# First phase of an adaLN transformer layer on Trainium2: what is loaded when, V projected four chunks behind Q and K, squares in four buffers

## The reference

```python
mod = (_silu(L0_c) @ L0_wmod).reshape(L0_c.shape[0], 6, 1, -1)
sa, ca, ga, sb, cb, gb = (mod[:, 0], mod[:, 1], ...)
h = _layernorm(x, axis=-1) * (1 + ca) + sa
q = hidden_states @ Wq + bq     # k, v alike; 8 heads of 128
scores = einsum('bhqd,bhkd->bhqk', q, k) / sqrt(HD);  attn = softmax(scores)
attn_out = attn @ v1 - lam * (attn @ v2)     # v1, v2: value heads 0..3 and 4..7
...
x = x + ga * _L0_attn_ref(h, ...)
x = x + gb * _L0_ffn_ref(_layernorm(x) * (1 + cb) + sb, ...)
```

## Time and profile before

| | |
|---|---|
| median of the runs shown | 2617.07 us (2615.12 to 2673.77, 3 runs) |
| the profiled execution | 2620.93 us |
| its span on the slowest core (core 3) | 2619.4 us |
| spans of the other cores | 2603.2 to 2617.3 us |
| TensorE busy | 2381.9 us, 91% of the span |
| VectorE, ScalarE, GpSimd busy | 27%, 54%, 12% |
| mean granted TensorE clock, core 3 | 0.971 of full speed |
| first score matmul, core 3 | 249.14 us |

### The profile page before, as it was taken

One profiled execution on the slowest core, in us unless ns is written; L12 is line 12 of the kernel. 1 busy time (PEld: TensorE's weight loads), 2 busy tenths in 40 slices (PEclk: granted clock), 3 DMA queues, 4 the chain that ended last, 5 costly groups with the idle time before them and its releaser, 6 DMA issues.

```text
span 2619.4 us, 43310 instructions; the slowest of 8 cores (2603.2 to 2619.4 us)
## 1 busy us (share of the span) xinstructions
PE 2381.9 (91%) x17364; PEld 1332.5 (51%) x17364; DVE 701.5 (27%) x1231; ACT 1422.8 (54%) x1551; POOL 319.1 (12%) x278
## 2 busy tenths in 40 slices
PE   1788999999989899989899995679999999999999
PEld 0343666655656565656566663334444444444444
DVE  2653121121222211122236666621020110201101
ACT  1333888978879688978887774451302113021120
POOL 1111000000000000000035453321010100101000
PEclk9999999999999899999999998899999999999999
DMA  9630101111011100000446666791020111202101
GB/s 219 143 97 1 22 9 26 22 25 22 9 25 21 25 5 9 5 9 7 71 106 142 146 149 174 188 210 52 33 81 17 65 33 49 81 14 67 33 33 41
DMA packets 119507, 162.74 MB, mean 62 GB/s; under 512 B 37696, under 2 KB 86924, under 8 KB 118288
## 3 DMA queue, kind: packets, MB, share of 16 engines
q1 hardware_dynamic: 79440, 119.60, 14.7%
q0 software_dynamic: 38672, 35.65, 9.9%
q10 hardware_dynamic: 1200, 4.72, 0.6%
...
## 4 chain that ended last, share of the span: by engine, by line
PE 80%; DMA 9%; DVE 4%; issue 3%; ACT 2%; another core or an unknown queue 1%; SPq 1%; POOL 0%; DVEq 0%; ACTq 0%; POOLq 0%
PE bk L191 41%; PE sc L191 38%; DMA aoR<-ao_scr 3%; DMA wms<-wmod 2%; DMA wm<-wmod 2%; DVE bst L673 1%; DMA Wo_sb<-Wo 1%; ACT h2T L198 1%; DMA xr<-x 1%; PE sc L195 1%; DMA x_scr<-xo 1%; SPq L64 0%; ACT expT L198 0%; PE bk L195 0%
## 5 line engine op out<-in xcount | busy, mean ns | idle before, releaser
L198 ACT ACTIVATE expT<-sc,Bneg 128x1024 bf16<-128x1024 f32 x1024 | 1096.5, 1117 | 223.3 <-PE sc L191 208.5
L191 PEld LDWEIGHTS bk<-v_aug,expT 128*128 128x128 bf16 x8192 | 553.0, 99 | 241.9 <-issue 27.8
L191 PE MATMUL bk<-v_aug,expT 128*128 128x129 bf16 x8192 | 645.2, 223 | 2.7 <-DVE rec L529 1.2
L191 PE MATMUL sc<-qS,kS 128*128 128x512 bf16 x2048 | 616.6, 383 | 1.3 <-ACT expT L198 0.4
L198 ACT ACTIVATE g<-sc,vecT 128x512 bf16<-128x512 f32 x256 | 176.0, 688 | 650.1 <-PE sc L191 650.1
L191 PE MATMUL sc<-h2F,w_sb 128*128 128x512 bf16 x2048 | 444.2, 380 | 0.0
L191 PEld LDWEIGHTS sc<-h2F,w_sb 128*128 128x128 bf16 x2048 | 200.6, 98 | 242.1 <-issue 1.1
L191 PE MATMUL bk<-hT,Wk_sb 128*128 128x512 bf16 x512 | 165.3, 413 | 10.3 <-DVE nmx L481 6.0
L191 PE MATMUL bk<-w2lo,g 128*128 128x512 bf16 x768 | 173.6, 379 | 0.0
L191 PE MATMUL bk<-w2hi,g 128*128 128x512 bf16 x768 | 173.6, 379 | 0.0
L191 PEld LDWEIGHTS sc<-qS,kS 128*128 128x128 bf16 x2048 | 156.0, 99 | 24.4 <-issue 12.6
(11 more groups left out here) (136 smaller groups left out, 1535.3 us busy)
## 6 DMA issues: line engine op xcount, KB each, us to landing
xr<-x SPq DMA_DIRECT2D x32, 512.0 KB, 7.3
xo<-x SPq DMA_DIRECT2D x32, 512.0 KB, 4.7
x_scr<-xo SPq DMA_DIRECT2D x32, 512.0 KB, 5.3
x1f<-x_scr SPq DMA_DIRECT2D x32, 512.0 KB, 4.9
out<-x1f SPq DMA_DIRECT2D x32, 512.0 KB, 3.7
...
w_sb<-w POOLq DMA_DIRECT2D x16, 512.0 KB, 8.4
```

Source lines behind the costliest of these rows:

```text
L191: return p.op("tensor", lambda e: e.matmul(out, lhsT, rhs, start=start, stop=stop, skip_group_check=True), waits, sig)
L198: return p.op("scalar", lambda e: e.activation(out, in_, fn, bias=bias, scale=scale), waits, sig)
```

## The change

The diff touches the first phase only, and one wait in the attention loop by its name.

- Loads. `wb` leaves the start and is issued by GpSimd in the fifth chunk (c = 4). x of every chunk but the first waits, through SP, for the fourth `wm1` quarter. Wv no longer comes on ScalarE's queue in two parts but on SP's in four of 1 MB, one behind each of the x loads of chunks 2 to 5.
- `Wvc` is combined two pieces at a time in chunks 1 to 4, behind the normalisation of that turn.
- `vproj` runs four chunks late: chunks 0 to 3 have none, V of chunks 0 to 3 is done in turns 4 to 7, and V of chunks 4 to 7 after the loop.
- Squares are made in `qkproj`, straight behind each evacuation, in four buffers. `norms1(c - 1)` opens turn c and has only the matmuls and the reductions; both heads use bank 6.
- `transpose1` uses banks 0, 1, 7 and 0; VectorE evacuates all but bank 1.
- The first transposes come ahead of the statistics of chunk 1.
- The two `bound` chains are stepped between the last V projections.

```diff
--- before.py
+++ after.py
@@ -130,7 +130,7 @@
...
-    sqA = [at("sqA%d" % i, CW, BF16, AO + 2048 + 1024 * i) for i in range(2)]
+    sqA = [at("sqA%d" % i, CW, BF16, AO + 2048 + 1024 * i) for i in range(4)]
...
@@ -239,8 +239,6 @@
     Wkd = Wk_d[:, :].rearrange("(k p) n -> p k n", p=128)
     p.dma("gpsimd", Wkv[:, :, 0:256], Wkd[:, :, 0:256], "wa")
     k_wa = p.dma("gpsimd", Wqv[:, :, 0:256], Wqd[:, :, 0:256], "wa")
-    p.dma("gpsimd", Wkv[:, :, 256:H], Wkd[:, :, 256:H], "wb")
-    k_wb = p.dma("gpsimd", Wqv[:, :, 256:H], Wqd[:, :, 256:H], "wb")
 
...
@@ -257,11 +255,13 @@
         for i in range(4):
             t = 4 * c + i
             x_tok[t] = p.dma("sync", xr[i][:, :], x_d[t * 128:(t + 1) * 128, :], "x%d" % i,
-                             [norm_tok.get(t - 4)])
+                             [norm_tok.get(t - 4), k_wm1[3] if c else None])
+
+    def wv_load(q):
+
+        p.dma("sync", wvv[:, 2 * q:2 * q + 2, :], Wvd[:, 2 * q:2 * q + 2, :], "wv%d" % q)
 
     x_load(0)
-    wvv = wv_st[:, :].rearrange("p (k n) -> p k n", k=KT)
-    Wvd = Wv_d[:, :].rearrange("(k p) n -> p k n", p=128)
 ...
@@ -321,10 +321,11 @@
 
     hT_tok = {}
     k_mod1 = [None]
+    TB = (0, 1, 7, 0)
 
     def transpose1(c):
         for kp in range(4):
-            b = kp % 2
+            b = TB[kp]
             for k2 in range(2):
                 kt = 2 * kp + k2
                 for i in range(4):
@@ -337,18 +338,22 @@
                 kt = 2 * kp + k2
                 dst = hT[:, kt * S + c * CW:kt * S + (c + 1) * CW]
                 src = bank_bf(b)[:, k2 * 512:(k2 + 1) * 512]
-                if b == 0:
+                if b != 1:
                     f = ts(dst, src, caT[:, kt:kt + 1], saT[:, kt:kt + 1], ALU.mult, ALU.add,
                            [k, k_mod1[0]])
                 else:
                     f = act(dst, src, AF.Identity, [k, k_mod1[0]],
                             bias=saT[:, kt:kt + 1], scale=caT[:, kt:kt + 1])
             free[b] = f
-            hT_tok[(c, b)] = f
+            hT_tok[(c, b == 1)] = f
 
     v_tok = {}
-    k_wvc = [None]
-    k_ones = [None]
+    k_wvc = {}
+
+    def wv_combine(q):
+        for kt in (2 * q, 2 * q + 1):
+            k_wvc[0] = stt(Wvc[:, kt * CW:(kt + 1) * CW], wvv[:, kt, CW:H], lamneg[:, 0:1],
+                           wvv[:, kt, 0:CW], ALU.mult, ALU.add, [p.last("wv%d" % q), k_lam])
 
     def vproj(c):
         for i in range(4):
@@ -372,21 +377,23 @@
                   waits, sig=kt == KT - 1)
 
     kq_tok = {}
-    sq_free = [None, None]
-    nrm_in = {}
+    sq_free = [None] * 4
+    sq_tok = [None] * 4
 
     def qkproj(c):
         n = 0
         for h in range(2):
-            for w, (W, dst, col) in enumerate(((Wk_sb, kS[h], C_BK), (Wq_sb, qS[h], C_BQ))):
+            for W, dst, col in ((Wk_sb, kS[h], C_BK), (Wq_sb, qS[h], C_BQ)):
                 b = 4 + n % 2
                 for kt in range(KT):
                     k = proj_mm(b, W, h, c, kt, [free[b], k_wa, hT_tok[(c, 0)], hT_tok[(c, 1)]]
                                 if kt == 0 else ())
-                free[b] = act(dst[:, c * CW:(c + 1) * CW], bank(b), AF.Identity,
+                src = dst[:, c * CW:(c + 1) * CW]
+                free[b] = act(src, bank(b), AF.Identity,
                               [k, k_wm1_used], bias=vecT[:, col + h:col + h + 1])
                 kq_tok[h] = free[b]
-                nrm_in[(c, h, w)] = (dst, free[b])
+                sq_tok[n] = tt(sqA[n][:, :], src, src, ALU.mult, [free[b], sq_free[n]],
+                               eng="gpsimd")
                 n += 1
 
     def norm_mm(b, sq, w, waits):
@@ -396,12 +403,10 @@
     def norms1(c):
         for h in range(2):
             for w in range(2):
-                dst, ev = nrm_in[(c, h, w)]
-                src = dst[:, c * CW:(c + 1) * CW]
-                ks = tt(sqA[w][:, :], src, src, ALU.mult, [ev, sq_free[w]], eng="gpsimd")
-                sq_free[w] = k = norm_mm(6 + h, sqA[w], w, [ks, free[6 + h]])
-            free[6 + h] = p.op("vector", lambda e, h=h: e.reduce_max(
-                nmx[h][:, c:c + 1], bank(6 + h), axis=AXX), [k])
+                n = 2 * h + w
+                sq_free[n] = k = norm_mm(6, sqA[n], w, [sq_tok[n], free[6]])
+            free[6] = p.op("vector", lambda e, h=h: e.reduce_max(
+                nmx[h][:, c:c + 1], bank(6), axis=AXX), [k])
 
     bneg_tok = {}
 
@@ -423,36 +428,48 @@
         bneg_tok[h] = ts(Bneg[:, h:h + 1], bnd[r][:, 3:4], -1.0, None, ALU.mult, waits=[k])
         yield
 
+    wvv = wv_st[:, :].rearrange("p (k n) -> p k n", k=KT)
+    Wvd = Wv_d[:, :].rearrange("(k p) n -> p k n", p=128)
+    LAG = 4
     stats1(0)
     norm1(0)
-    p.dma("scalar", wvv[:, 0:4, :], Wvd[:, 0:4, :], "wv0", [k_wm1[1]])
-    p.dma("scalar", wvv[:, 4:8, :], Wvd[:, 4:8, :], "wv1", [k_wm1[1]])
     x_load(1)
-    stats1(1)
     cp(saT[:, :], bank(6)[:, 0:8], [k_wm1_used])
     k_mod1[0] = free[6] = ts(caT[:, :], bank(6)[:, 8:16], 1.0, None, ALU.add)
     transpose1(0)
-    for kt in range(KT):
-        k_wvc[0] = stt(Wvc[:, kt * CW:(kt + 1) * CW], wvv[:, kt, CW:H], lamneg[:, 0:1],
-                       wvv[:, kt, 0:CW], ALU.mult, ALU.add,
-                       [p.last("wv0"), k_lam] if kt == 0 else [p.last("wv1")] if kt == 4 else ())
-    k_ones[0] = memset(v_aug[:, :].rearrange("p (t c) -> p t c", c=129)[:, :, 128:129], 1.0,
-                       [k_wvc[0]], sig=True)
+    stats1(1)
     norm1(1)
     for c in range(NC):
-        vproj(c)
         if c >= 1:
             norms1(c - 1)
+        qkproj(c)
         if c + 1 < NC:
             transpose1(c + 1)
-        qkproj(c)
         if c + 2 < NC:
             x_load(c + 2)
+            if c < 4:
+                wv_load(c)
             stats1(c + 2)
             norm1(c + 2)
+        if 1 <= c <= 4:
+            wv_combine(c - 1)
+            if c == 4:
+                k_ones = memset(v_aug[:, :].rearrange("p (t c) -> p t c", c=129)[:, :, 128:129],
+                                1.0, [k_wvc[0]], sig=True)
+                p.dma("gpsimd", Wkv[:, :, 256:H], Wkd[:, :, 256:H], "wb")
+                k_wb = p.dma("gpsimd", Wqv[:, :, 256:H], Wqd[:, :, 256:H], "wb")
+        if c >= LAG:
+            vproj(c - LAG)
     norms1(NC - 1)
-    for h in range(2):
-        for _ in bound(h, 6 + h):
+    vproj(NC - LAG)
+    gens = [bound(0, 6), bound(1, 7)]
+    for c in range(NC - LAG + 1, NC):
+        for gen in gens:
+            for _ in range(3):
+                next(gen, None)
+        vproj(c)
+    for gen in gens:
+        for _ in gen:
             pass
 
 
@@ -514,7 +531,7 @@
             k = mm(bk[b][:, off:off + 129], expT[g % 3][:, j * 128:(j + 1) * 128],
                    v_aug[:, kt * 516 + (h % 4) * 129:kt * 516 + (h % 4 + 1) * 129],
                    first, kt == NT - 1,
-                   ([exp_tok[g], v_tok[NT - 1], k_ones[0]] if j == 0 else [])
+                   ([exp_tok[g], v_tok[NT - 1], k_ones] if j == 0 else [])
                    + ([free[4 + b]] if first else []),
                    sig=last or j == 7)
             if last:
```

## The result

The changed kernel takes 2644.93 us, the median of four executions (2640.52, 2640.59, 2649.26, 2981.47); those of the kernel before in the same comparison took 2615.12, 2617.07, 2673.77 and 2903.13, median 2645.42. The last of the first four and the last two of the others had one or both halves of the chip at a lower clock for most of the kernel, and every ratio leaves such executions out: the others have medians of 2640.59 and 2616.10 and a ratio of **1.0105, 95% interval 1.0058 to 1.0151**, so the change makes the kernel 1% slower. The forecast was 2645, 1.1% slower. That it meets 2644.93 to a tenth is luck: with the execution of 2981.47 counted, the median falls halfway between 2640.59 and 2649.26.

A forecast was written before the change was run, and what follows sets the result against it. TensorE was taken as the bound, with waits ahead of the first score matmul. That matmul moves from 249.14 to 279.2 us, + 30.1, less 1.5 in attention: + 28 on the median 2617.07 gives 2645 us, range 2628 to 2660.

The forecast's parts named there:

- 2.3 us for each restart of TensorE: First phase: matmuls restarting after an idle run at a lower clock, losing 2.3 us each time, bounds 0 and 2.8.
- 1.5 us gained behind the first score matmul: Start of attention: it begins at full clock instead of over 3 us at 0.50, saving 1.5 us.
- Step 1: Prologue loads: last modulation quarter at 41.7 us instead of 62.2, Q/K of chunk 0 at 55.5 us.
- Rival (b): Prologue: shared HBM sets the weights' landing, so little is gained; Q/K(0) near 70 us, total 2660 us; chance 0.08.
- Step 2: Chunk loop: TensorE waits some 11 us per turn for VectorE's reduction; turns 20.8 or 22.15 us, plus 2.3 restart.
- Rival (a): Chunk loop: the reduction doesn't hold TensorE up and the change works as drawn, 2562 us; chance 0.05.
- Rival (c): First phase: restarts at the lower clock cost nothing or are mostly covered by VectorE, 16 us less, 2629 us; chance 0.12.

The follow-up runs named there:

- loads_back: The changed kernel with only its loads put back to the old ones; one comparable execution, 2657.21 us.
- two_banks: The changed kernel with a bank for each head's norms again and transposes back in banks 0, 1, 0, 1; ratio 1.0011 to the kernel before.
- combo5: The changed kernel with statistics before transposes, two norm banks, four transpose banks, nmA behind hT evacuations; ratio to the kernel before 0.9876, repeated 0.9859.
- after_again: The changed kernel unaltered, run once more beside the kernel before; ratio 1.014, profiled execution 2651.36 us.

## Why the prediction was right in its mechanism and wrong in sizes

**In short.** The direction, the wait that causes it and the place of every stall came as written. What failed is the size of two terms: 2.3 us for each restart of TensorE, 16.1 for seven, where core 6 shows 1.3 to 2.2, 11.6 for seven; and 1.5 us gained behind the first score matmul, where the cores gained 4.9 on average. On the mean of the eight cores the change costs 21.5 us, not 28.

**Step 1, the prologue: right, by two errors that cancel.** 41.7 was predicted for the last modulation quarter, and 42.1 to 44.2 came on the eight cores (42.42 on core 6); 55.5 for Q/K(0), and 54.1 to 56.4 came. But the price of 140 packets per us, taken while x's tail was on the engines, did not hold for the other 1694. On core 6 the queue, now without x beside it, sent 1426 packets from 27.1 to 36.0 us, 160 per us, so that the last of the 4096 left near 38 instead of 39.2, and the matmuls followed some 4.5 us later instead of 2.5. Rival (b), Q/K(0) at 70, is excluded, and `loads_back` shows the 20 us going when the loads go back.

**Step 2, the turn: right in kind, a little dear.** Ends of the transposes, predicted and on core 6:

| | predicted | measured |
|---|---|---|
| transposes 1 | 67.3 | 67.3 |
| transposes 2 | 90.4 | 89.5 |
| transposes 3 | 114.9 | 113.2 |
| transposes 4 | 139.3 | 137.2 |
| transposes 5 | 163.7 | 161.0 |
| transposes 6 | 196.1 | 193.2 |
| transposes 7 | 224.4 | 220.9 |
| first score matmul | 279.2 | 273.7 |

The first turn took 22.2 instead of 23.1, those with combines 23.7 to 24.0 instead of 24.45, those with V 32.2 and 27.7 instead of 32.4 and 28.3. The idle time of about 11 us, its releaser, and V(0) behind the Wvc combine (11.5 us after the transposes predicted, 11.5 measured) came as written. Rival (a), that the reduction doesn't hold TensorE up, is excluded by every turn. That VectorE keeps its order, read off and stated in the Trainium skill, "TensorE: Matmul & The Clock Gate", in the row on engine queue depth, carries to ScalarE in `two_banks`: `kS`, ready near 71, went at 76.93.

**The step that failed: the size of the restart.** The prediction put 2.3 us on each. Q/K(1) behind the 10.09 us wait ran from 78.80 to 87.03, 8.23 us against 6.9 at full speed: 1.3. Behind 11.41, 11.81 and 11.42 it was 1.5, 1.4 and 1.5, and 1.5 in Q/K(0). V(0) and the second half of V(1) lost 2.2 each. That makes 11.6 us for seven restarts instead of 16.1. On the other cores Q/K(1) to Q/K(4) lost 0.9 to 2.1. Behind shorter waits in `combo5` it could be more: 2.7 us behind a wait of 4.01 (104.12 to 113.68). All of it stays inside the bounds of 0 to 2.8, and nothing here gives a rule by which to choose within them. Rival (c), restarts for nothing, is wrong.

Smaller terms went both ways. VectorE's stretch up to the reduction was 2.4 us shorter over the four turns than priced, and the two norm matmuls with the gap behind them 2.7 us longer (1.06 us a turn instead of 0.4, as they are the first work behind the wait). Q/K(0) had a wait of 1.52 us for ScalarE that the sum didn't have, which a start 0.6 us sooner and the cheaper restart hid.

**The tail and attention.** From transposes 7 to the first score matmul it took 52.8 us instead of 54.8, as the bound matmuls hide fully and V ran a little closer. The sum was also counted from core 3 of the kernel before, 249.14, the last of its eight cores; their mean is 247.35. Attention gained more than the 1.5 us given: from the first score matmul to the end the cores took 2363.0 us on average before and 2358.1 after, and again 2358.1 in `after_again` and 2356.7 in `loads_back`, so this is no accident of one execution. The first 3 us had a granted clock of 1.00 on all eight cores after, and 0.50 on all eight before. Behind the first score matmul the stretches at 0.50 add up to 136 us before and 125 after on average; at half speed, 10 us less of them is an estimated 5 us, about what was gained. Why the later ones are fewer is open.

So + 26.4 us at the first score matmul for the predicted + 30.1, and - 4.9 for - 1.5: + 21.5 on the mean span, where + 28 was forecast. The comparison's ratio says 1.05% of 2617, + 27.5, with an interval of + 15 to + 40, and its medians + 24.5 (2640.59 against 2616.10). The forecast's 28 agrees with the ratio in part because the slowest of eight cores counts, which the sum had from one core, and in part by luck.

**What the prediction left out.** Costed at nothing were the Wv loads, `wb`, x and the squares, and rightly so (`wb` landed 26.6 us after its issue, 26 predicted). It did not see that taking the wait on `nmx` away would uncover one in ScalarE's queue; that did not matter for this change, but `two_banks` fell 0.8% short by it.
